# Image patches fetched chunk by chunk, the embedding formed in masked matmuls, staged rows kept in idle buffers, and a second pair of score banks

## The reference

```
embed_w  = prelu(conv1x1(x, Wa, ba), aa)         # 32 channels, full size
match_in = prelu(conv1x1(x, W1, b1), a1)         # 16 channels, full size: the queries
raw_w    = extract_patches(embed_w, 6, 2)        # 576 patches 6x6: the values
ref      = prelu(conv1x1(mean2x2(x), W2, b2), a2)
w        = extract_patches(ref, 3, 1)            # 576 keys of 16*9
wn       = w / max(norm(w), 1e-4)
xp       = extract_patches(match_in, 3, 1)       # 2304 queries of 16*9
yi       = softmax(10 * einsum(wn, xp), over the 576 keys)
yt       = transposed_conv(yi, raw_w), stride 2
yd       = (conv3x3(yt, Wd, stride 2) + bd) / 6
x        = x + yd
```

## Time and profile before

| | us |
|---|---|
| median of 3 runs | 233.08 (232.84 to 234.24) |
| the profiled execution, whole | 233.31 |
| its span, first to last instruction | 231.5 |
| busy PE / DVE / ACT / POOL | 184.0 / 143.1 / 118.7 / 118.5 |
| mean granted TensorE clock | 0.865 of full |

### The profile page before, as it was taken

The page is one execution under the profiler, slowest core; times in us unless marked ns, Lnnn a source line. Parts: engine busy times, 40 slices in busy tenths (PEclk is TensorE's granted clock), DMA queues, the critical chain, the costliest instruction groups (busy, mean ns, idle before and its releaser), DMA issues.

```text
span 231.5 us, 3433 instructions
## 1 busy us (share of the span) xinstructions
PE 184.0 (79%) x1094; PEld 146.5 (63%) x1094; DVE 143.1 (62%) x291; ACT 118.7 (51%) x217; POOL 118.5 (51%) x105
## 2 busy tenths in 40 slices
PE   0396549209697984996999979999978999799993
PEld 0342539209374973884888858877856876578790
DVE  5669875303588688278265676566679379678301
ACT  4876614304999835474456646655555336224300
POOL 8352220000787997848929398998578950000000
PEclk9999556656999797699799999999999999999555
DMA  5290179882113000444533201144035100002413
GB/s 151 52 224 13 21 121 155 110 155 73 33 36 62 4 0 6 81 78 82 151 101 91 43 0 30 34 81 73 3 79 125 50 3 0 1 0 54 76 28 52
DMA packets 16552, 14.68 MB, mean 63 GB/s; under 512 B 9590, under 2 KB 14262, under 8 KB 16342
## 3 DMA queue, kind: packets, MB, share of 16 engines
q1 hardware_dynamic: 15046, 13.42, 29.8%
q10 hardware_dynamic: 1488, 1.04, 1.6%
HBM read 2.14 MB, written 1.18 MB: 14 GB/s over the span
## 4 chain that ended last, share of the span: by engine, by line
PE 50%; DVE 21%; ACT 8%; SPq 8%; issue 6%; DMA 4%; ACTq 1%; DVEq 0%
PE yt L934 13%; PE zt L918 10%; PE ps L892 10%; SPq L524 7%; DVE negm L1416 3%; ACT nt L1124 3%; DVE v L1477 3%; PE zt L954 3%; PE ps L918 3%; DMA vl<-mimg 2%; DVE mst L1317 2%; DVE yf L1433 2%; DVE mimg L1352 2%; DMA par<-params 2%; SPq L517 2%
## 5 line engine op out<-in xcount | busy, mean ns | idle before, releaser
L709 POOL TENSOR_TENSOR nt<-nt 128x599 f32<-128x599 f32 (+1 forms) x51 | 69.7, 1366 | 42.5 <-ACT nt L1132 38.2
L934 PE MATMUL yt<-yf,kf 125*128 125x384 f32 (+1 forms) x120 | 50.8, 508 | 2.7 <-DVE yf L1433 2.7
L918 PEld LDWEIGHTS zt<-ident,nt 128*125 128x125 f32 (+1 forms) x300 | 40.3, 182 | 11.9 <-issue 3.1
L1124 ACT ACTIVATE nt<-ps,negm 128x576 f32<-128x576 f32 x31 | 23.0, 741 | 41.6 <-DVE negm L1416 41.6
L918 PE MATMUL zt<-ident,nt 128*125 128x128 f32 (+1 forms) x300 | 42.7, 280 | 0.0
L1416 DVE TENSOR_REDUCE negm<-ps 128x1 f32<-128x576 f32 x31 | 23.4, 755 | 18.7 <-PE ps L892 18.5
L1132 ACT ACTIVATE nt<-nt,rps 128x599 f32<-128x599 f32 x36 | 28.6, 795 | 7.1 <-DVE rps L1423 7.0
L892 PE MATMUL ps<-wh,vh 128*128 128x288 f32 x62 | 18.6, 384 | 12.1 <-ACT nt L1124 8.4
L892 PEld LDWEIGHTS ps<-wh,vh 128*128 128x128 f32 x62 | 10.7, 211 | 19.2 <-ACT nt L1124 15.7
L934 PEld LDWEIGHTS yt<-yf,kf 125*128 125x128 f32 (+1 forms) x120 | 19.2, 197 | 3.9 <-DVE yf L1433 3.3
L1433 DVE COPY yf<-zt 125x384 f32<-125x384 f32 (+1 forms) x28 | 19.4, 693 | 3.5 <-issue 2.6
(11 more groups left out here) (171 smaller groups left out, 322.1 us busy)
## 6 DMA issues: line engine op xcount, KB each, us to landing
nt<-nt SPq DMA_DIRECT2D x12, 285.2 KB, 3.3
vh<-mimg SPq DMA_DIRECT2D x14, 72.0 KB, 2.6
vl<-mimg SPq DMA_DIRECT2D x14, 72.0 KB, 2.5
vh<-mimg SPq DMA_DIRECT2D x8, 120.0 KB, 5.2
vl<-mimg SPq DMA_DIRECT2D x8, 120.0 KB, 4.9
emb<-emq SPq DMA_DIRECT2D x32, 18.8 KB, 1.8
v<-x SPq DMA_DIRECT2D x2, 288.0 KB, 3.9
v<-vr SPq DMA_DIRECT2D x2, 288.0 KB, 5.1
```

What stands on the lines that cost most here:

```text
L709: pool.tensor_tensor(nt[:, dst, (to + 1) * KP + 1:(to + 1) * KP + 1 + n], nt[:, one, (row1 + 1) * KP + 1:(row1 + 1) * KP + 1 + n], nt[:, o ...
L918: last = nc.tensor.matmul(turned(sums_bank(m), n, column), keys_at(tile, r + dr, n, shift), ident[:, :], start=at == 0, stop=at == len(wor ...
L934: nc.tensor.matmul(yt[:, k % 2, 0:CHUNK], kf[b][0:n, blk, :], yf[0:n, blk, :], start=blk == 0, stop=blk == KB - 1).then_inc(s_mb, 1)
L1124: nc.scalar.activation(strided(nt[:, tile_of(g, jb), :], KP + 1, (KP * HL // 2, 2), (KP, HL // 2), (1, WL)), strided(scores_of(t)[:, 0, :] ...
```

## The change

- Image 0's patches are fetched chunk by chunk, six DMAs each, with a semaphore for each chunk. SP issues chunks 0 to 3, then `row_after`(0), then chunks 4 and 5. The ninth tap of a chunk is two DMAs instead of three; ACT issues those of chunks 0 to 2, SP the rest.
- The embedding is formed in place. `wa4` grows to 224 columns with zeros around the weights; each of the two jobs is now eight matmuls, four accumulated into each of two halves of a bank. `emq` and the 32 DMAs of `embedding` are gone. DVE clears `wa4` (896 columns) and `emb` (600) at the start where it cleared `emq` (600).
- Image 1's staged rows have eight slots: two of `mst`, four in `yf`, two in `kf` of image 1. Its `conv1` jobs run in steps 1 to 8, and the split (`match`) in steps 9 to 12. ACT's `match_high` does nothing for image 1: DVE makes the high half too, with a `tensor_scalar_mul`, one in front of each subtraction. Copies into `yf` of block 1 and above wait for six splits, the copy into `kf` of image 1 for eight.
- From tile 19 (DOUBLE) odd tiles go to `pm`, and PE again makes tile s+2 in step s, waiting for the exponential of tile s. All small products of `pm` therefore lie before step 17: the embedding of image 1 is in steps 12 and 13 (before: 21 and 22), its turning in step 15 (28 and 29), the inverse norms in step 10 (14 and 15).
- `residual` moves from step 12 to the end of the work in front of the steps.

```
+DOUBLE = 19
+WIDE = 7 * C
+STAGES = 6
...
 IM2COL = len(SHIFTS) + 3
+NINTH = [(2 * CR, 0), (CR, 2 * CR)]
...
     ("conv1", 0, (7,)), ("match", 0, (6, 7)), ("inorm", 0, (0, 1)), ("mean", 1, (0,)), ("dup", 0, (0,)), ("keys", 0, (0, 1)),
-    ("after", 0, (0,)), ("ninth", 0, (0, 1)), ("weights", 1, (0,))]
+    ("after", 0, (0,)), ("ninth", 0, (0, 1, 2)), ("weights", 1, (0,)),
+    ("residual", 0, (0,)), ("residual", 1, (0,))]
 SPREAD = [
     ("wst", 0, 1, 0, 1), ("bias_2", 1, 1, 0, 1), ("bias_1", 1, 1, 0, 1), ("conv2", 1, 2, 1, 1), ("bias_a", 0, 1, 2, 1),
-    ("emb", 0, 2, 4, 1), ("conv1", 1, 8, 7, 3), ("match", 1, 8, 7, 3), ("squares", 1, 1, 9, 1), ("dup", 1, 1, 29, 1),
-    ("after", 1, 1, 30, 1), ("norm", 1, 1, 20, 1), ("ek", 0, 2, 30, 1), ("residual", 0, 1, 36, 1), ("residual", 1, 1, 37, 1),
-    ("inorm", 1, 2, 42, 3), ("keys", 1, 2, 45, 3), ("wst", 1, 1, 57, 1), ("bias_a", 1, 1, 61, 1), ("emb", 1, 2, 65, 3),
-    ("ek", 1, 2, 85, 3),
+    ("conv1", 1, 8, 4, 3), ("squares", 1, 1, 6, 1), ("emb", 0, 2, 12, 6), ("norm", 1, 1, 17, 1), ("wst", 1, 1, 24, 1),
+    ("match", 1, 8, 24, 1.5), ("ek", 0, 2, 27, 1), ("bias_a", 1, 1, 28, 1), ("inorm", 1, 2, 30, 1), ("dup", 1, 1, 35, 1),
+    ("after", 1, 1, 36, 1), ("emb", 1, 2, 36, 3), ("keys", 1, 2, 42, 2), ("ek", 1, 2, 45, 1),
...
 BEHIND_PE = {
-    "act": {"conv2": 1, "conv1": 1, "emb": 1, "ek": 1, "match": 4, "dup": 8, "after": 8},
+    "act": {"conv2": 1, "conv1": 1, "emb": 1, "ek": 1, "dup": 5, "after": 5},
     "dve": {"bias_2": 1, "bias_1": 1, "bias_a": 3, "conv2": 3, "conv1": 3, "emb": 3, "norm": 2, "inorm": 2, "keys": 2,
-            "match": 7, "dup": 7},
+            "match": 3, "dup": 3},
...
         wsf = sb("wsf", [C, 4 * C])
-        wa4 = sb("wa4", [128, 4, C])
+        wa4 = sb("wa4", [128, 4, WIDE])
...
             mimg = tmp("mimg", [96, BLOCKS * BLOCK], F32R)
-            emq = tmp("emq", [128, HL * KP])
...
         s_after = sems("columns_after_copied")
-        s_emb = sems("embedding_in")
...
+        def four_emptied(eng):
+            for n in range(nfour - 4, nfour):
+                wait_emptied(eng, *plan[n])
         def group(eng, name, b, i):
...
-        def ninth(eng, n, low, t, many=1):
-            src = F(mimg[64 + low:64 + low + CR, :])
-            at = src.offset + match_rows_at(1 + SHIFTS[2][0], t + 2, 0)
-            return eng.dma_start(F(vr[CR * n:CR * (n + 1), CHUNK * t:CHUNK * (t + many)]),
-                                 bass.AP(src.tensor, at, [[mimg.shape[1], CR], [BLOCK, many], [1, CHUNK]]))
+        def ninth(eng, rows, first, t):
+            at = match_rows_at(1 + SHIFTS[2][0], t + 2, 0)
+            return eng.dma_start(F(vr[first:first + rows, CHUNK * t:CHUNK * (t + 1)]), F(mimg[64:64 + rows, at:at + CHUNK]))
         def arrived(eng, landed, g, images):
-            together = 16 * (3 if landed is s_vr else sum(n for _, n in SHIFTS))
-            if images == 1:
-                eng.wait_ge(landed[min(g, 1)], together if g else 48)
-            else:
-                eng.wait_ge(landed[g], (96, together + 48, 48)[min(g, 2)])
+            eng.wait_ge(landed[g], 16 * (len(NINTH) if landed is s_vr else len(SHIFTS)) * images)
         def patches_in(eng, images):
-            for g in range(NCH if images > 1 else 2):
+            for g in range(NCH):
...
         def scores_of(t):
-            return zt if t < FILL and t % 2 else ps
+            if t % 2 == 0 or FILL <= t < DOUBLE:
+                return ps
+            return zt if t < FILL else pm
         def tile_of(g, jb):
...
                           .rearrange("k (p l) -> k p l", l=W)).then_inc(s_out, 16)
+        def stage(b, i):
+            slots = [mst[:, 0, :], mst[:, 1, :]]
+            if b:
+                wide = yf[0:96, :, :].rearrange("p k w -> p (k w)")
+                slots += [wide[:, L + HALF * n:L + HALF * (n + 1)] for n in range(4)]
+                wide = kf[b][0:96, :, :].rearrange("p k c -> p (k c)")
+                slots += [wide[:, HALF * n:HALF * (n + 1)] for n in range(2)]
+            return slots[i % len(slots)]
+        def staged_free(eng, i):
+            if i < 2:
+                eng.wait_ge(s_msp[0], ROWS - 1 + i)
         def copied_by_act(k, blk):
...
-            def match_patches(b, t, many=1):
+            def match_patches(b, t):
...
                 pitch = mimg.shape[1]
-                cols = slice(CHUNK * t, CHUNK * (t + many))
...
                         src = F(mimg[32 * k + low:32 * k + low + CR, :])
-                        at = src.offset + match_rows_at(1 + dx, t, 0)
-                        if many == 1:
-                            sp.dma_start(F(dst[3 * CR * k:3 * CR * k + n * CR, cols]),
-                                         bass.AP(src.tensor, at, [[pitch, CR], [BLOCK, n], [1, CHUNK]])).then_inc(done, 16)
-                        else:
-                            for row in range(n):
-                                to = F(dst[3 * CR * k + row:3 * CR * k + row + 1, cols])
-                                wide = dst.shape[1]
-                                to = bass.AP(to.tensor, to.offset, [[n * wide, CR], [1, CHUNK * many]])
-                                sp.dma_start(to, bass.AP(src.tensor, at + BLOCK * row,
-                                                         [[pitch, CR], [BLOCK, many], [1, CHUNK]])).then_inc(done, 16)
-                if b:
-                    for n, low in enumerate((0, CR, 0)):
-                        ninth(sp, n, low, t).then_inc(s_vr[t], 16)
-            def embedding(b):
-                wait_emptied(sp, "emb", b, 1)
-                if b:
-                    sp.wait_ge(s_mf, misc_no["ek", b - 1, 1] + 1)
-                for n in range(4):
-                    size = HL // 4 * KP
-                    for q in range(4):
-                        sp.dma_start(emb[C * n:C * (n + 1), size * q:size * (q + 1)],
-                                     emq[C * q:C * (q + 1), size * n:size * (n + 1)]).then_inc(s_emb[b], 16)
+                        src = bass.AP(src.tensor, src.offset + match_rows_at(1 + dx, t, 0), [[pitch, CR], [BLOCK, n], [1, CHUNK]])
+                        sp.dma_start(F(dst[3 * CR * k:3 * CR * k + n * CR, CHUNK * t:CHUNK * (t + 1)]), src).then_inc(done, 16)
+                if b or t >= NCH // 2:
+                    sp.wait_ge(s_zero, 3)
+                    for rows, first in NINTH:
+                        ninth(sp, rows, first, t).then_inc(s_vr[t], 16)
             def output_weights():
...
             ref_patches(0)
-            match_patches(0, 0)
-            match_patches(0, 1, NCH - 1)
+            for t in range(4):
+                match_patches(0, t)
...
             row_after(0)
-            embedding(0)
+            match_patches(0, 4)
+            match_patches(0, 5)
...
             match_patches(1, 3)
-            embedding(1)
...
                         wait_emptied(pe, *plan[n - 4])
+                elif n < nfour + 2:
+                    four_emptied(pe)
                 elif n < ntail:
-                    wait_emptied(pe, *plan[max(n - 2, nfour - 1)])
-                elif n == ntail:
-                    wait_emptied(pe, *plan[ntail - 2])
-                    wait_emptied(pe, *plan[ntail - 1])
+                    wait_emptied(pe, *plan[n - 2])
...
                 v = x4[b][:, :].rearrange("p (i u j v) -> p i u j v", u=2, j=WL, v=2)
-                for k in range(2):
-                    last = nc.tensor.matmul(o[:, REFQ * k:REFQ * (k + 1)], wa4[:, :, :].rearrange("p q c -> p (q c)"),
-                                            v[:, :, i, :, k], start=True, stop=True)
+                for r in range(2):
+                    for n in range(4):
+                        at = C * (3 - n)
+                        last = nc.tensor.matmul(o[:, REFQ * r:REFQ * (r + 1)], wa4[:, 2 * i + r, at:at + 128],
+                                                v[:, :, n // 2, :, n % 2], start=n == 0, stop=n == 3)
...
             def embed_turned(b, i):
-                pe.wait_ge(s_emb[b], 16 * 16)
+                wait_emptied(pe, "emb", b, 1)
...
             def scores(t):
...
                 b, i = g // NCH, g % NCH
-                if t > 1:
-                    pe.wait_ge(s_ex, t - 1 if t < FILL else t)
+                if t == DOUBLE:
+                    wait_emptied(pe, *plan[ntail - 2])
+                    wait_emptied(pe, *plan[ntail - 1])
+                elif t > 1:
+                    pe.wait_ge(s_ex, t if FILL <= t < DOUBLE else t - 1)
...
                     if k == 0:
-                        wait_emptied(pe, *plan[nfour - 1])
+                        four_emptied(pe)
...
                     scores(s + 2)
-                if FILL <= s + 1 < NT:
+                if FILL <= s + 1 < DOUBLE:
                     scores(s + 1)
+                if DOUBLE <= s + 2 < NT:
+                    scores(s + 2)
...
             def match_high(b, i):
+                if b:
+                    return
...
```

(39 more changed lines are left out.)

## The result

The changed kernel takes 224.31 us (median of 4 runs, 222.69 to 225.94) against 233.04 for the kernel before beside it (232.84 to 234.24): a ratio of 0.9615, 95% interval 0.9521 to 0.971. The forecast was 220.5 with a range of 212 to 229, so the sign, the range and most of the size were right; 3.8 us of the gain did not come. The profiled execution took 225.59 us, 223.8 of them its span. A second series gave 224.64. Medians here are of all executions of a kernel, while a ratio leaves out those more than 1.5% above the fastest of the same kernel (one of the kernel before took 900.24 us), so a ratio can differ from the quotient of two medians.

A forecast was written before the change was run, and what follows sets the result against it. Bounds in turn: SP queue to tile 3, ACT to 10, DVE mostly to 18, then PE, with the DCT last. Marks 45.5, 63.7, 92.9, 105.9, 164.5 plus 54.0 gave span 218.5; with 1.8 outside, 220.3, rounded to 220.5; range 212 to 229.

The forecast's parts named there:

- To tile 3: Start to tile 3's exponential: PE's 8.19 us wait goes, 2 us more from its clock; 45.5 instead of 55.69.
- Rival 4: Before tile 3: small DMAs land late in full engines, chunk 1 after 46, 5 us gone; 225.5 us, chance 0.06.
- Tiles 3 to 9: ACT's stretch: 16.84 less 2.6 roundings, plus 1.0 `slanted` and 3.0 embedding stalls, 18.2 us; tile 9 at 63.7.
- if the stalls at the embedding jobs are over 3 us each: Sign of being wrong: ACT's waits for PE's two embedding jobs, taken as 1.5 us each, exceed 3 us each.
- Tiles 9 to 14: DVE's stretch with all eight splits: pairs at 1.75, 14.0 us, edge copies 5.0; 29.2 us in all, tile 14 at 92.9.
- four edge copies, 1.25 each: DVE between tiles 9 and 14: 5.0 us, priced between the median and the maximum of their row.
- rival 1: Steps 9 to 12: POOL holds DVE at every turn, pairs 2.98 us, edge copies 1.65; 232 to 236 us, chance 0.16.
- Rival 2: Steps 9 to 13: DVE nearly free of POOL, pairs at 0.9 us; 215 us in all, chance 0.22.
- Tiles 14 to 18: PE late: a step of one tile, 5/3 of a turn and values block, 3.24 us; four make 13.0, tile 18 at 105.9.
- Tile 18 to step 35: PE's stretch: 56.1 us of work plus 2.5 of waits, 58.6 instead of 65.8; step 35 at 164.5.
- over 95% busy with no wait for the exponential: Sign of being right: PE's state from tile 18 on, with step 35 near 164.5.
- Rival 3: Image 1: POOL becomes the bound with 53.4 us of sums and pairs, price 4; 224.5 us, chance 0.13.

The follow-up runs named there:

- p1: Kernel before with only image 0's vh and vl patches, chunks 1 to 5, fetched chunk by chunk with a semaphore each; 224.81 us (0.9692).
- c0: Changed kernel with image 0's chunks 1 to 5 on one semaphore again, ahead of `row_after`(0); 236.28 us (1.0166).
- c2: Changed kernel with nine of POOL's sums of image 0 in steps 9 to 14 cut to 8 columns; 220.45 us (0.9485).
- a2: Changed kernel with ACT making the high half of image 1's rows again, slots and steps kept; 219.46 us (0.9358).
- a0: The changed kernel once more, with no edit, as the measure for its group; 224.64 us (0.966).
- a1: Changed kernel with DOUBLE = 36, a single pair of score banks from tile 11 to the end; 227.74 us (0.975).
- a3: Changed kernel with image 0's two embedding jobs behind the `conv1` job of their step instead of ahead; 222.66 us (0.9598).
- b1: Changed kernel with image 0's two joins of a pair in different steps; 225.01 us (0.9715).
- b3: Changed kernel with the edits of a2, a3 and b1 together; 219.22 us (0.9471).
- c1: a2 with image 0's embedding formed as in the kernel before, its 16 DMAs on SP behind chunk 5; 225.54 us (0.9622).
- c3: c1 with the 16 embedding DMAs ahead of chunks 4 and 5; 220.18 us (0.9467).

## Why the forecast was right, and where it missed

The span came out 5.3 us longer than the forecast's 218.5, and the profiled execution stood 1.3 above the median. The forecast's own sum, with the 0.2 us that it names taken off, is 220.1; the 220.5 is rounded up. Stretch by stretch:

| stretch | forecast | measured | difference |
|---|---|---|---|
| to tile 3 | 45.5 | 45.73 | +0.2 |
| tile 3 to 9 | 18.2 | 20.26 | +2.1 |
| tile 9 to 14 | 29.2 | 24.95 | -4.3 |
| tile 14 to 18 | 13.0 | 17.06 | +4.1 |
| tile 18 to step 35 | 58.6 | 61.47 | +2.9 |
| to the end | 54.0 | 54.33 | +0.3 |

The misses partly cancel: 9.6 us too little in five stretches, 4.3 too much in one. That the time lies well inside the range is thus in part luck.

**To tile 3: right**, by the steps given. Taking off the 8.19 us of the earlier trace rows and 2 us for a PE that keeps its clock is what happened; SP issues chunk 3 by 43.6 us in the kernel after. That this is the part that carries the change is shown from both sides, by p1 and by c0. Rival 4, late small DMAs, is refuted.

**Tiles 3 to 9: the stall was mis-sized.** "I take 1.5 of stall twice, 3.0" measured 3.64 + 2.10 = 5.74. The second job was underrated by 0.6; the first ran at 1.2 GHz, which the forecast named as its upper bound and did not take. The mark moved by 2.1 us and not by 2.7, because the kernel before had 0.97 us of waits of its own on ACT in this stretch (0.67 and 0.30), which are gone, against two new ones of 0.17. The other two terms were off by as much each way: ACT loses five roundings there and not six, and gains one `slanted` of the embedding and not two. With these the sum is 20.3. By the forecast's own sign ("if the stalls at the embedding jobs are over 3 us each") this part was half wrong.

**Tiles 9 to 14: the pair was right, the edge copies were not.** 1.65 against 1.75 a pair, and c2 shows that the reason given, DVE held by POOL, is the true one. "four edge copies, 1.25 each" measured 0.47 each: they were priced between the median and the maximum of a row in which POOL ran beside image 1's copies, but now POOL was idle most of the time beside them (POOL's timeline of the kernel after, below), for want of scaled tiles, since DVE itself was late. That is the feedback that rival 1 named against itself; it took out the 3 us and kept that rival away. Rival 2, pairs at 0.9, did not come either, but c2 shows its mechanism: with POOL's sums short a pair takes 1.13, and tile 14 comes 5.0 us earlier.

```profile
87.89 1.25 POOL L710 TENSOR_TENSOR nt<-nt 128x599 f32<-128x599 f32 x1 [2.32 <-ACT nt L1141]
```

In a2, where DVE reaches the edge copies while POOL's sums still run, the first two of them cost 1.53 and 1.31 us, as the forecast had it. The Trainium skill, SBUF — State Buffer, section "SBUF: two separate sides", describes an exclusive lock on a port pair for which a VectorE instruction with two SBUF inputs competes with GpSimd, whichever starts first. The trace agrees with who wins: 0.46 us when DVE began 0.01 us ahead, 1.63 us when it began behind. That the one-input `tensor_scalar_mul` in float32 is held as well (0.97 and 1.07 against 0.35) agrees too, if it runs in a two-port mode, which no row here can show.

**Tiles 14 to 18: the step that failed.** "From tile 14 to 18 PE is late next ... four of them 13.0" left out what else hangs there. PE's timeline of the kernel after:

```profile
89.94 2.21 PE L845 MATMUL pm<-x,wa 128*128 128x144 f32 x16
...
98.05 1.25 PE L856 MATMUL pm<-wdf,emb 128*125 128x128 f32 x10
...
103.89 0.91 PE L939 MATMUL yt<-yf,kf 125*128 125x384 f32 x2 [0.92 <-DVE yf L1451]
```

The second embedding job of image 1, its turning and a wait for the copy into `yf` make 2.2 + 1.1 + 0.9 = 4.2 us, as much as the whole difference. The forecast put both embedding jobs under the cover of the splits in steps 12 and 13 ("where PE waits for DVE; if it did not wait, it would cost 4.8"). One of the two was not covered, because DVE was done sooner than said; and the turning in step 15 had no term at all. The runs part the two. In the changed kernel and seven others (a0, a1, a3, b1, b3, c1, c2) the stretch takes 17.05 to 17.08 us, whether tile 14 stands at 85.13 (b3) or at 93.78 (c1): it is PE's own work and one wait. In c3 DVE's maximum of tile 14 comes so late that PE does the second job meanwhile, and there the stretch takes 15.08 (PE's, then DVE's timeline of c3):

```profile
86.09 2.21 PE L863 MATMUL pm<-x,wa 128*128 128x144 f32 x16
```
```profile
88.05 0.76 DVE L1454 TENSOR_REDUCE negm<-ps 128x1 f32<-128x576 f32 x1
```

So some 2 us of the 4.3 won before tile 14 and the 4.1 lost behind it are one error, the job that a later DVE would have covered. The other 2, the turning and the wait, were missing from the sum in any case.

**Tile 18 to step 35: waits mis-sized.** "I take 2.5" for what stays of the waits measured 4.3, three of the four at pieces of joins. The forecast had read the 8.4 us of the earlier trace rows as lying mostly in this stretch. In the trace of the kernel before only 3.6 of them do (1.65, 0.47 and 1.51), and with 0.46 for a ninth tap its waits there are 4.1. So against the kernel before the waits have not shrunk. The stretch is 4.3 us shorter because PE's work is (61.69 us busy before, 57.17 now), and the second pair keeps the waits from growing to the 5.5 of a1. The loop worked out for two tiles in flight (2.9 us against two steps of 3.24 each) was right where no join lies; the joins add up to 2.77 us to it. The rest, 1.1 us, is PE's own work (57.10 busy against 56.1). b1 shows that moving the joins gives 2.2 us at step 35 and less than 1 at the end. The forecast's sign "over 95% busy with no wait for the exponential" was not met: PE is 93% busy and waits three times. Rival 3, POOL as the bound, did not come: POOL is 50.89 busy of 61.4 and PE never waits for a POOL result there.

**What the sum hid.** The forecast had the change as one gain with costs. The runs give it parts: the fetch by chunk 8.4 us (p1, 233.23 to 224.81, and as much by the spans; 7 by the ratio); all the rest except DVE's high halves some 4 to 5 more (p1's 224.81 to a2's 219.46, from two groups whose kernel before stood 0.15 apart; by the spans of the profiled executions 223.1 to 219.2); DVE's high halves 5 back (219.46 to 224.64). By the ratios each of these last two is some 2 us larger. Of the 4 to 5, some 2.8 are the bank pair's (a1). What the eight slots bring was not tried alone, so the remaining 1 to 2.5 stay undivided between them, the embedding and the moved jobs. The forecast's sentence "DVE has taken in the matches that ACT did, and all at once" was the right warning, with no alternative priced: ACT is 10.83 us busy of 25 between tiles 9 and 14, and had room for eight roundings of 0.43.

## What to carry to other kernels

One semaphore over a batch of transfers makes the first consumer wait for the last one; splitting it can outweigh everything else in a change, even when the smaller transfers are slower to issue in all. Before moving an instruction from one engine to another, look at both in the very stretch: here the engine with the lower share there was the better place, and an instruction that VectorE does in 0.35 us alone may cost 1.0 beside GpSimd. And when a stretch is forecast by its bounding engine, work out the floor of the second engine too: what the first gains beyond that floor can come back as a loss in the next stretch.

## What the runs showed of the hardware

- In the kernel after, a float32 `tensor_scalar_mul` of 96x288 from SBUF to SBUF took 0.34 to 0.37 us free and 0.68 to 1.07 when held by POOL. The subtraction with two SBUF operands took 0.45 free and 1.60 to 1.66 behind the start of a POOL sum or pair, ending about 0.3 us after it in all four cases. A join of 32x376, also two SBUF operands, took 0.6 free (1.24 or 1.25 for two) and up to 1.88 beside POOL (b1).
- Who starts first decides: DVE's subtraction at 74.25, 0.01 us ahead of POOL's sum at 74.26, was not slowed, and neither was the one at 84.01, 0.13 us ahead of a sum. Then the sum is the one that is held: the one at 84.14 took 1.43 us where others of its size take 1.25. A start that differs by a tenth of a microsecond cost or saved 1.2 us here.
- Idle time of PE went with a lower clock behind it. Between 74 and 86 us of the kernel after, where PE waits for DVE, the granted clock was 0.72 and the embedding job took 3.20 us instead of 2.21; in a2 the same job, behind a hole of 2.17 us, took 3.80.

```profile
74.00:86.00 12.00, 8.85 (x42) 8.34 (x43) 11.63 (x21) 4.68 (x10) 10.34 (x7) 0.72 0.00 1
```
